# Two middle convolutions of a four-layer kernel: where the bias, the sum, the statistics and the sample kernels are computed

## The reference

```python
# layer 0: q, k, v (3x3 convolutions), a 7x7 convolution as bias, softmax over channels
attn = jnp.einsum('bchw,bcjw->bchj', q, k) / d + bias
out  = jnp.einsum('bchw,bcjw->bchj', v, jax.nn.softmax(attn, axis=1))
# layer 1: 3x3 convolution of int8-valued numbers
out = lax.conv_general_dilated(qx, qw, ...) * (sx * sw / (MAXV * MAXV))
return out + bias.reshape(1, -1, 1, 1)
# layer 2: a 3x3 kernel of its own for each sample and channel
pooled = x.mean(axis=(2, 3))
kernels = (relu(pooled @ w1 + b1) @ w2 + b2).reshape(b, NK, K, K)
out = depthwise_conv(x, kernels)
# layer 3: 21x21 filters of eight directions, weighted with a local variance
```

## Time and profile before

| what | value |
|---|---|
| median of three runs | 1413.55 us (1412.29 to 1417.16) |
| profiled execution | 1413.83 us, span 1412.0 us |
| PE busy | 1170.5 us, 83% |
| DVE busy | 893.7 us, 63% |
| ACT busy | 560.6 us, 40% |
| POOL busy | 573.7 us, 41% |
| mean granted clock of PE | 0.879 |

### The profile page before, as it was taken

How to read it: one execution, slowest core, us unless ns; L and a number is a source line. 1 busy time by engine, 2 the same in 40 slices (tenths; PEclk the granted TensorE clock), 3 DMA queues, 4 the chain that set the end, 5 groups by cost and what they waited for, 6 DMA issues and landing times.

```text
span 1412.0 us, 38547 instructions
## 1 busy us (share of the span) xinstructions
PE 1170.5 (83%) x16376; PEld 796.3 (56%) x16376; DVE 893.7 (63%) x1103; ACT 560.6 (40%) x722; POOL 573.7 (41%) x463
## 2 busy tenths in 40 slices
PE   0489999999999999992354486599988999999897
PEld 0478999999999999992211243111113444444343
DVE  5444657575858574737699487799984455435353
ACT  4643455545455545332352485355541111111010
POOL 2045464646464746453164586488870000000000
PEclk9989999999999999997666599655558999999998
DMA  7302020202010101000011133000024454554554
GB/s 103 70 2 66 3 64 4 58 10 54 14 47 22 36 3 35 4 3 1 27 52 46 34 111 86 16 0 0 0 74 102 109 143 133 143 133 111 145 138 93
DMA packets 130232, 81.04 MB, mean 57 GB/s; under 512 B 95761, under 2 KB 119602, under 8 KB 129074
## 3 DMA queue, kind: packets, MB, share of 16 engines
q1 hardware_dynamic: 130098, 78.99, 22.4%
HBM read 36.42 MB, written 11.99 MB: 34 GB/s over the span
## 4 chain that ended last, share of the span: by engine, by line
PE 44%; SPq 20%; DVE 16%; issue 10%; POOL 3%; ACT 3%; DMA 3%; DVEq 1%; POOLq 0%; ACTq 0%
PE psum L1427 35%; SPq L486 12%; SPq L475 3%; SPq L493 3%; DVE small L819 2%; DMA edge_columns<-arena 2%; ACT arena L1061 2%; POOL arena L1335 2%; PE psum L1455 2%; PE psum L1447 2%; DVE arena L915 1%; DVE arena L909 1%; DVE arena L831 1%; DVE arena L922 1%; DVE small L925 1%
## 5 line engine op out<-in xcount | busy, mean ns | idle before, releaser
L1427 PE MATMUL psum<-arena 128*128 128x64 f16 (+2 forms) x11904 | 513.5, 207 | 43.6 <-ACT arena L1061 40.5
L1427 PEld LDWEIGHTS psum<-arena 128*128 128x128 f16 x11904 | 496.6, 99 | 59.1 <-issue 40.8
L607 DVE TENSOR_TENSOR arena<-psum,arena 128x512 f32<-128x512 f32 x128 | 87.6, 690 | 196.9 <-PE psum L1427 168.1
L1620 PE MATMUL psum<-arena 128*128 128x480 f16 (+2 forms) x960 | 196.5, 366 | 3.6 <-DVEq L122 2.0
L1271 POOL TENSOR_TENSOR arena<-arena 128x256 f16<-128x256 f32 x64 | 51.3, 801 | 326.6 <-ACT arena L1055 326.6
L1620 PEld LDWEIGHTS psum<-arena 128*128 128x128 f16 x960 | 94.2, 98 | 104.6 <-issue 5.1
L1632 PE MATMUL psum<-arena 128*128 128x512 f16 x576 | 133.2, 392 | 17.7 <-DMA arena<-edge_columns 17.7
L1275 POOL TENSOR_SCALAR arena<-arena,constants_f 128x256 f16<-128x256 f16 x128 | 138.3, 1108 | 0.0
L1051 ACT ACTIVATE arena<-arena 128x256 f16<-128x256 f32 x64 | 26.7, 417 | 228.6 <-issue 127.8
L1632 PEld LDWEIGHTS psum<-arena 128*128 128x128 f16 x576 | 57.3, 101 | 91.4 <-issue 15.3
L953 DVE TENSOR_TENSOR arena<-arena 128x1024 f16<-128x1024 f32 x16 | 19.6, 1226 | 131.3 <-ACT arena L1226 131.3
(11 more groups left out here) (186 smaller groups left out, 1779.3 us busy)
## 6 DMA issues: line engine op xcount, KB each, us to landing
arena<-edge_columns SPq DMA_DIRECT2D x160, 80.0 KB
arena<-in_filter_tables SPq DMA_DIRECT2D x8, 1280.0 KB, 6.0
X<-in_x SPq DMA_DIRECT2D x64, 128.0 KB, 3.1
arena<-arena SPq DMA_DIRECT2D x32, 256.0 KB, 4.0
out<-X SPq DMA_DIRECT2D x64, 128.0 KB, 2.5
arena<-arena SPq DMA_DIRECT2D x48, 132.0 KB, 2.5
arena<-arena SPq DMA_DIRECT2D x32, 140.0 KB, 2.6
arena<-arena SPq DMA_DIRECT2D x16, 280.0 KB, 2.7
```

The costliest lines, as they stand in the source:

```text
L607: v.tensor_tensor(out_, bank_rows(k), biasrow, ALU.add).then_inc([g.staged0, g.staged1][k], 1)
L1427: last = mm(conv[k][:, c0:c1], win[:, kk, lx, y + e, dx:dx + W, :].rearrange("p w s -> p (w s)"), wt[:, lw, d, w0:w1], start=(n == 0), sto ...
L1620: mm(bank[4 * s + 2 * f + hf][:, C * lo:C * hi], tb[:, f, d + 2, lt], xt[s][:, hf, lx, YP + d + lo:YP + d + hi].rearrange("p y c -> p (y c)"),
```

## The change

- Layer 0's result is added to X together with layer 1's bias (one `scalar_tensor_tensor` in place of one `tensor_tensor`); the means and extremes are corrected by the bias where layer 1's scale is computed, and two tiny instructions move behind the one that ACT waits for.
- Layer 1's result is scaled and added to X by DVE straight from PSUM (`add1`); ACT's dequantise, the tile d1 and POOL's addition go. POOL clamps partitions 96 to 127; DVE keeps 0 to 95. DVE's list is round(n), add1(n-3), clamp(n), statistics(n-3) (LAG = 3), written out without a hardware loop.
- The statistics are joined straight into mvall; the copy goes. Their partial results alternate between two tiles.
- Layer 2's kernels are split into f16 and remainder once for all samples (three small DVE instructions); DVE then spreads both halves of a sample with one instruction of 768 f16 elements. POOL's two instructions and ACT's one on the kernels go. DVE's list is spread(n), remainder(n), add2(n-3), statistics(n-3).
- PE is released into a PSUM slot by the sum (x2_sum, x3_sum), no longer by d1 or by the statistics; its part of the first nine samples' statistics comes ahead of convolution 11.

```diff
@@ add_attention
-                    v.tensor_tensor(xs, xs, tp[k].rearrange("p (y w s) -> p s y w", y=4, s=2), ALU.add
+                    v.scalar_tensor_tensor(xs, tp[k].rearrange("p (y w s) -> p s y w", y=4, s=2), bias1, xs, ALU.add,
@@ DVE, statistics and layer 1
+                part = (bn, bn0)[n % 2]
+                v.wait_ge(summed, n + 1 + NS)
...
-                link(v.bn_aggr(mv[:, 0:2], bn[:, 0:12]))
-                v.tensor_copy(mvall[:, bass.ds(2 * n, 2)], mv[:, 0:2]).then_inc(done, 1)
+                link(last)
+                v.bn_aggr(mvall[:, 2 * n:2 * n + 2], part[:, 0:12]).then_inc(done, 1)
...
-                for p0, p1, e in ((0, 96, 0), (96, P, 1)):
-                    v.tensor_scalar(a12[p0:p1, k, 0, e:e + NY, PAD1:PAD1 + W], y12[p0:p1, k], MAGIC - QMAX, MAGIC,
+                v.tensor_scalar(a12[0:96, n % NS, 0, 0:NY, PAD1:PAD1 + W], y12[0:96, n % NS], MAGIC - QMAX, MAGIC,
...
+            def add1(n):
+                xb = X[:, n].rearrange("p y w -> p (y w)")
+                v.wait_ge(g.c1_done, n + 1 + free12["c1_done"])
+                v.scalar_tensor_tensor(xb, psum[:, 1024 * (n % NS):1024 * (n % NS) + 1024], one[4], xb,
+                                       ALU.mult, ALU.add).then_inc(g.x2_sum, 1)
+
+            for n in range(B + LAG):
+                if n < B:
+                    round1(n)
+                if n >= LAG:
+                    add1(n - LAG)
+                if n < B:
+                    clamp1(n)
+                if n >= LAG:
+                    sample_stats(n - LAG, g.x2_sum, g.x2_ready)
@@ DVE, layer 2
-            v.tensor_copy(kv.rearrange("p v b -> p (v b)"), tp[0][:, 0:12 * B]).then_inc(g.kv_ready, 1)
+            link(v.tensor_scalar(kv.rearrange("p v b -> p (v b)"), tp[0][:, 0:12 * B], KS, None, ALU.mult))
+            link(v.tensor_copy(kv16[:, :, 0, :], kv.rearrange("p v b -> p b v")))
+            link(v.tensor_tensor(kv16[:, :, 1, :], kv.rearrange("p v b -> p b v"), kv16[:, :, 0, :], ALU.subtract))
...
+                v.tensor_tensor(k2[:, n % NS].rearrange("p l (v c) -> p (l v) c", c=C),
+                                kv16[:, n].rearrange("p l v -> p (l v)").unsqueeze(2).broadcast_to([P, 24, C]),
+                                unit32.unsqueeze(1).broadcast_to([P, 24, C]), ALU.mult).then_inc(g.k2_ready, 1)
...
+            for n in range(B + LAG):
+                if n < B:
+                    spread_kernels(n)
+                    low2(n)
+                if n >= LAG:
+                    add2(n - LAG)
+                    sample_stats(n - LAG, g.x3_sum, g.x3_ready)
@@ ACT
-                a.activation(d1[:, k], psum[:, 1024 * k:1024 * k + 1024], ACT.Identity, scale=one[4], bias=bias1
...
-                a.wait_ge(g.kf, n + 1)
-                a.activation(k2[:, k, 0], k2f[:, k], ACT.Copy).then_inc(g.kh, 1)
@@ POOL
-                gp.tensor_tensor(xb, xb, d1[:, k], ALU.add).then_inc(g.x2_sum, 1)
+                gp.tensor_scalar(a12[96:P, k, 0, 1:1 + NY, PAD1:PAD1 + W], y12[96:P, k], MAGIC - QMAX, MAGIC,
+                                 ALU.max, ALU.subtract).then_inc(g.q1_pool, 1)
...
-                gp.tensor_tensor(k2f[:, k].rearrange("p (v c) -> p v c", v=12), kb.broadcast_to([P, 12, C]),
...
-                gp.tensor_tensor(k2[:, k, 1], k2f[:, k], k2[:, k, 0], ALU.subtract).then_inc(g.kl, 1)
```

More of the change, by code:

```diff
@@ L45 @@
 NSUM = 2
+LAG = 3
 KB, KQ, KV, KK = range(4)
@@ L824, in quantise, with sample_stats @@
-            def quantise(i, k):
-                n = NS * i + k
+            def sample_stats(n, summed, done):
+                xb = X[:, n].rearrange("p y w -> p (y w)")
+                part = (bn, bn0)[n % 2]
+                v.wait_ge(summed, n + 1 + NS)
+                wait_reuse(v, done, n - 1)
+                for h_ in range(2):
+                    last = v.bn_stats(part[:, 6 * h_:6 * h_ + 6], xb[:, 512 * h_:512 * h_ + 512])
+                link(last)
+                v.bn_aggr(mvall[:, 2 * n:2 * n + 2], part[:, 0:12]).then_inc(done, 1)
@@ L834, in finish1 @@
-            def finish1(i, k):
-                n = NS * i + k
-                wait_alone(v, g.x2_sum, n + 1 + free12["x2_sum"])
-                sample_stats(n, g.x2_ready)
-            for k in range(NS):
-                quantise(0, k)
-            with v.Fori(1, B // NS) as i:
-                link.loop(i - 1, 8)
-                for k in range(NS):
-                    quantise(i, k)
-                    finish1(i - 1, k)
-            link.end(B // NS - 1)
-            for k in range(NS):
-                finish1(B // NS - 1, k)
+                v.tensor_scalar(a12[0:96, n % NS, 0, 0:NY, PAD1:PAD1 + W], y12[0:96, n % NS], MAGIC - QMAX, MAGIC,
+                                ALU.max, ALU.subtract).then_inc(g.q1_ready, 1)
@@ L880, in _ @@
-            for k in range(NS):
-                prepare2(0, k)
-            last2 = B // NS - 1
-            with v.Fori(1, last2) as i:
-                link.loop(i - 1, 12)
-                for k in range(NS):
-                    prepare2(i, k)
-                    finish2(i - 1, k)
-            link.end(last2 - 1)
-            for k in range(NS):
-                prepare2(last2, k)
-                finish2(last2 - 1, k)
-                if k == 0:
-                    assert NS * (last2 - 1) == NT
-                    v.wait_ge(g.x3_ready, NT + 1 + free12["x3_ready"])
+            link(v.tensor_scalar(kv.rearrange("p v b -> p (v b)"), tp[0][:, 0:12 * B], KS, None, ALU.mult))
@@ L898, in _ @@
                     set_scale(scale3, shift3, g.l3_scale)
-            for k in range(NS):
-                finish2(last2, k)
             def row_sums(i, k):
@@ L1566, in conv2 @@
                 last.then_inc(g.c2_done, 1)
[L1568 to L1575 removed]
+            at2 = (NT + LAG) // NS
+            each_sample(pe, 0, at2, conv2)
+            for n in range(NS * at2, B):
+                if n == NT + LAG:
+                    all_stats(2, bank[0])
+                if n == NT + NS:
+                    pe.wait_ge(g.gst_var, 3)
+                conv2(at2 if n < NS * (at2 + 1) else at2 + 1, n % NS)
             def sums(i, k):
```

136 lines of the change are left out of this document (53 added, 83 removed).

## The result

| | before | after |
|---|---|---|
| median | 1414.5 us (4 runs) | 1395.8 us (4 runs, 1393.2 to 1396.8) |
| ratio | 1 | 0.9864 (0.9842 to 0.9887) |
| profiled execution, span | 1413.8, 1412.0 | 1396.8, 1395.0 |
| layer 1, first rounding to next statistics | 88.07 | 74.41 |
| from there to the copy of kv | 10.57 | 10.57 |

The change is faster by 1.4%; 1422.0 was forecast, 0.6% slower. The page of the changed kernel: busy time of the engines, and POOL's clamp, which is new.

The account below looks back on a forecast made before the run. DVE's list, with POOL's hold of the shared access, was taken to bound layers 1 and 2. The profiled 1413.8 + 13.2 (layer 1) - 4.9 (layer 2) gave 1422.1 us, range 1389 to 1437.

Parts of the forecast that it names:

- What bounds the kernel: Layers 1 and 2: DVE's list sets the time, lengthened by POOL's hold of the shared access; PE waits for windows.
- The copy's 0.84: Layer 1's copy into mvall, 0.84 us on average against 0.16 to 0.18 of other tiny instructions: not all work.
- POOL's clamp holds DVE off to its end: Layer 1: DVE's clamp waits until POOL's clamp ends, so a sample costs 2.96 + T us.
- the collision at 744: Layer 1 before: POOL's addition, 743.79 to 746.64, met two DVE clamps lasting 3.44 us; 2.17 read as lost.
- T: Time of POOL's new 32x1024 clamp in layer 1: 3.1 us chosen, each 0.1 worth 1.6 us of the kernel.
- the upper bound, 3.96: T from POOL's 256-element multiplication with no fixed part: 3.96 us, making layer 1 115.1, 27 more than before.
- Rival B: Layer 1: POOL's clamp hides under the sum or does not hold DVE; layer 70.4, kernel 1391 us, chance 0.18.
- my own sum: Layer 1: three first samples, 13 of 2.96 + T, three tails of 3.04: 51.7 + 16 T, 101.3 us.
- The sum out of PSUM does not collide: Layer 1: DVE's sum, with one input in SBUF, is not held by POOL; 1.36 us to the statistics.
- Layer 2: Period 5.3 us in place of 4.88, earlier first sum at 810.2, end at 890.0: 4.9 less than 894.87.
- Between and behind: Between the layers: small instructions added and removed, inside 1 us, counted below; no loss put behind layer 2.
- the likeliest case: Whole kernel with T of 2.8 to 3.6 us: 1417 to 1430, chance 0.45.

Follow-up runs that it names:

- run 5: The kernel before, with POOL adding only 256 of each sample's 1024 elements in layer 1: 1399.4 us, ratio 0.9895; layer 1 71.15.
- run 6: Changed kernel with both layer 1 clamps on DVE, none on POOL, plus a useless two-input POOL addition per sample: 1413.7 us, ratio 0.9995; layer 1 90.65.
- run 2: The changed kernel with both clamps of layer 1 on DVE and none on POOL: 1398.5 us, ratio 0.9884; layer 1 76.5.
- run 3: The changed kernel with POOL's layer 1 clamp replaced by a two-input subtraction, lower clamp there left out: 1398.1 us, ratio 0.9888; layer 1 77.6.
- run 9: The changed kernel with POOL's layer 1 clamp cut to one subtraction, lower clamp there left out: 1390.5 us, ratio 0.9823; layer 1 69.2.
- run 1: The probe, a kernel of its own: POOL's candidate instructions alone, then some beside streams of tiny DVE instructions; clamp 3.63 us alone, no kernel time or ratio.
- run 11: Changed kernel with both layer 1 window parts on ACT, lower clamp left out, and POOL's first layer 3 squares held until DVE's row sums: 1390.1 us, ratio 0.9825.
- run 7: The kernel before, without layer 1's copy into mvall, DVE's list written out, partial results alternating between two tiles: 1410.5 us, ratio 0.9979; layer 1 84.34.

## Why the prediction was wrong, by its steps

**What bounds the kernel:** right. DVE's list sets both layers, and POOL's two-input instructions lengthen it. Runs 5 and 6 show it from both sides: most of the hold taken away, layer 1 is 16.9 us shorter; a hold put back that nobody waits for, layer 1 is 14.1 longer than in run 2. The copy's 0.84 was read rightly as well (0.20 in run 5).

**"POOL's clamp holds DVE off to its end":** this is the step that failed. I had two rows of evidence, a free DVE instruction at 139.77 and a longer one at 140.71, and took the second, since it agreed with the collision at 744 and since DVE's clamp is a scalar instruction like it. The rest of that time line of before, in which these two are the second and the fifth of five DVE instructions, says something else:

```profile
139.42 0.31 DVE L558 TENSOR_TENSOR small<-small 128x2 f32<-128x2 f32 x1 [0.30 <-DVE small L557]
...
139.96 0.30 DVE L560 TENSOR_SCALAR small<-small 128x2 f32<-128x2 f32 x1
140.30 0.37 DVE L561 TENSOR_TENSOR small<-small 128x2 f32<-128x2 f32 x1
...
141.12 0.67 POOL L1276 TENSOR_TENSOR arena<-arena 128x256 f16<-128x256 f32 x1
141.24 0.56 DVE L591 TENSOR_TENSOR small<-small 128x2 f32<-128x2 f32 x1
```

Beside the two multiplications (139.25 to 141.19) five DVE instructions get through, four of them stretched by 0.1 to 0.3. None is kept for the 1.0 that a multiplication lasts, and they come one after the other in a chain, each behind the last; with a hold to the end two or three would have fitted. The row that I took, at 140.71, does end with its multiplication (141.21 and 141.19), so by itself it fitted. Only the one at 141.24 meets a two-input instruction, and it ends with that, at 141.8. And the collision at 744 had two inputs on POOL's side. In the steady part of layer 1 the same DVE clamp loses 0.85 beside the two-input instruction (run 3), 0.24 beside the two-constant clamp and nothing beside the one-step instruction (run 9), though POOL's clamp is twice as long as its two-input instruction (3.95 and 1.90).

What the runs show in place of a hold to the end is a hold in parts: 0.87 at the beginning of the probe's clamp, 0.72 and 0.85 in the 4.77 of POOL's first clamp in the changed kernel, with free instructions between. In the steady part I take these parts to fall beside DVE's sum and statistics, since neither is lengthened and only 0.24 a sample is lost; no run shows where they fall. I had taken all of T to be lost but for the 1.2 of the sum: a sample was to cost 2.96 + 3.1 = 6.06, and it costs 4.03. I also had POOL's clamp begin as the rounding ends; in the steady part it begins 1.6 later (rounding until 714.90, POOL from 716.48), behind its own predecessor.

By the Trainium skill (SBUF — State Buffer, Who interferes with whom) whoever comes first has the shared ports for the whole instruction. The probe's two-input rows agree (2.37, 2.34, 2.34 until POOL's end); its one-input clamp does not, with 0.87 of 4.93 held, and there the measurement decides.

**The size of T:** 3.1 was chosen; the instruction takes 3.63 alone and 3.99 in the kernel. My 3.4 from 3.2 ns an element was nearer than what I chose, and two steps do cost more than one (3.63 against 2.77). That the upper bound, 3.96, meets 3.99 is luck: it has no fixed part, while run 1 has four clamps of 512 elements in 7.88 and four of 1024 in 14.69, which leaves some 0.3 fixed in each, and 0.36 of the 3.99 is what DVE's instructions add in the kernel. With the hold as I had it, 3.99 would have made layer 1 51.7 + 63.8 = 115.5 us; it is 74.4. The two errors pull in opposite directions, the first being much the larger. Without a hold to the end T still acts as the length of POOL's own queue: 16 x 3.99 = 63.8, back to back from 695.81 to 760.77 (65.0 with the gaps), which with 0.9 ahead of it and 8.5 behind it is all of the 74.4. Rival B had this layer at 70.4 with no hold, and 1391 in all. Its sample was even a little long (4.16 for 4.03). What it lacked are the ends of the layer: DVE does nothing for 5.9 us until the first convolution is there (706.99), and the last three samples take 10.7 (758.64 to 769.30) where 9.1 was put. No term of my own sum had that first wait either.

**The sum out of PSUM does not collide:** right; it takes 1.28 beside POOL's addition in run 6 and 1.21 beside its remainder in layer 2.

**Layer 2:** 4.9 less predicted, 5.65 measured. The first sum comes 25.8 us behind layer 1's end (26.5 said), the mean period between the first and the ninth sum is 5.21 (5.3 said), the spread is 0.90 (0.9 said). But the period is made of other terms: undisturbed it is 4.66, not 5.1, for from the sum to the statistics it is 1.25 (815.64 to 816.89) where I had 1.36, from there to the spread 1.44 (816.89 to 818.33) where I had 1.68, and the spread and the remainder each begin some 0.1 before the one ahead of them is shown to end, where I had added durations; and POOL's remainder costs 0.55 in mean, not 0.2, as 1.9 at once in two samples of the eight and 0.7 in a third. Two errors of opposite sign again. Two more lie behind them: the chain of nine samples' statistics takes 6.0 (839.60 to 845.55) where I had put 4, and the last four samples 11.5 (863.38 to 874.84) where I had 12.2. So from the first sum to the end it is 79.7 with 79.8 said, which is partly luck. The clock was said to stay at 1.00; it is 0.90 between 811 and 846, and with DVE as the bound little hangs on it.

**Between and behind:** nothing between the layers, as said. That POOL would be at layer 3's first squares before DVE came to its row sums (1.6 us) wasn't thought of; it follows from POOL's list being shorter. Run 11 shows that the wait tried there doesn't bring it back.

**The range** from 1389 to 1437 holds 1395.8 only because it reached to rival B, which had 0.18; the likeliest case, 1417 to 1430, was slower than before, and the kernel is faster.

## What to carry to other kernels

Ask of every POOL instruction not how long it is but how long it keeps DVE out, and price the two apart: in these runs two inputs keep a DVE instruction that wants the shared access out to their end, one input with constants for a part. When a row for and a row against stand beside each other, place both inside the instruction they are to speak of before choosing. A DVE instruction that reads PSUM and one tile can stand where POOL's two-input work runs (1.28 and 1.21, its usual length); put it there, and keep chains of tiny instructions away (2.7 us lost in run 11). And a tiny instruction that is five times longer than its like is not the cost but the place where the cost shows: removing it moves the hold on (run 7: it was busy for 13.4 us, the layer is 3.7 shorter, and the clamps and roundings are 10.6 longer).

## What the hardware showed beyond that

- Behind its first 0.87 us POOL's one-input clamp gives way to a stream of tiny DVE instructions, and not they to it: 4.93 us beside a stream of one-input ones, its last 0.89 behind the stream's end; 3.63 alone.
- With arithmetic, a one-input instruction on POOL is the longer one: 3.63 with two constants and 2.77 with one, against 2.3 for two inputs on the same tile. On 128 partitions it is as long as on 32, 14.71 against 14.69 for four.
- In the first run a cast of the same 32x1024 takes 1.0 us on POOL and makes a DVE instruction of 0.18 take 1.05 to 1.08, the same 0.9 us of hold as the clamp, which is 3.5 times as long. That the hold is the reading of the one input would fit both; it is not shown.
- Not settled: which phases of a one-input instruction hold DVE. The probe shows the clamp's first 0.87 us held. In the changed kernel one part lies just ahead of the end (the rounding at 699.60 loses 0.85 and ends at 701.13, so it gets in near 700.4, and POOL ends at 700.58), and another, at 696.95, comes 1.1 behind the recorded start, after two DVE instructions that followed each other without a gap. A part of some 0.9 at the beginning and one at the end, with either engine waiting for the other, would fit all of it; but no run separates the two, and beside the two-input stream of run 1 the end held nothing. The 0.1 to 0.3 beside the multiplications of layer 0 may be another such part. Whether it is the number of inputs as such that decides wasn't tried beyond these forms.
